# A 6,250-step LSTM on one core: the input projections added by narrow products over four column tiles

## The chip, the cores and the metric

The kernel runs on one core of a Trainium2 chip. The metric is the device time of one execution in microseconds; lower is better. Time before: 31,179.84 us, the median of 3 runs (31,170.26 to 31,184.28).

## The reference

The program is a stack of four layers on 6,250 nodes with 256 features, each added to its input: a weighted graph aggregation, a mixture of eight experts, a graph attention with four heads, and an LSTM over the nodes in order. Only the LSTM matters here:

```python
def _lstm(x, W_ih, W_hh, b_ih, b_hh):
    x_proj = jnp.einsum('btd,gd->btg', x, W_ih) + b_ih + b_hh
    def step(carry, xp):
        h, c = carry
        gates = xp + h @ W_hh.T
        i, f, g, o = jnp.split(gates, 4, axis=-1)
        c = jax.nn.sigmoid(f) * c + jax.nn.sigmoid(i) * jnp.tanh(g)
        h = jax.nn.sigmoid(o) * jnp.tanh(c)
        return ((h, c), h)
    _, hs = jax.lax.scan(step, (h0, c0), jnp.swapaxes(x_proj, 0, 1))
```

The batch is 1, there are 6,250 steps, h and c have 256 elements and each step needs 4 x 256 gate values. All of it is f32. `x_proj` is computed for all steps beforehand.

## The kernel before

The program runs its stages one after the other; the last three are `stage_project` (it writes all projections to HBM), `stage_lstm` and `stage_finish`. The change is in `stage_lstm` alone.

`stage_lstm` gives each engine its own instruction stream, with a hardware loop over N // PER passes (N = 6,250). PER = CH * LU = 2 * 5 = 10 steps are written out in each pass, so there are 625 passes. The order within a step is set by semaphores only; the values they are compared with are computed from the loop's register `i`.

- Layout. The 256 elements of h are held as two columns of 128 (`ht`, index `c`). A gate's 256 values are made as four pieces of 64 (`j`), each piece on a PSUM partition that is a multiple of 32. The gates f, i with g, and o have a PSUM bank each, with two sets of banks that alternate by step (`s = k % 2`).
- SyncE loads the projections of five steps at a time (40 rows of `xp`, two buffers `b`), when TensorE has said by `xp_used` that the buffer has been read.
- TensorE (L1152 to L1180) first adds the projections into the three banks with one product each (L1160). The weights are `sel[:, u, :]`, a matrix of 128 x 128 zeros and ones that picks the rows of step `u`; the moving operand is 64 columns of `xp`. It has ones only in columns 32 j and 32 j + 1. `start=True` makes this product overwrite the bank. Then TensorE waits for h of the step before (`h_ready`) and adds the recurrent part with narrow products: the weights are one or two columns of `ht`, the moving operand is 64 columns of `w`, and `tile_position=(0, 32 * j)` puts each on one of four column tiles of the array. There are 8 for f (L1167), 16 for i and g (L1173) and 8 for o (L1178), and after each group `gates_ready` is counted up.
- VectorE (L1225 to L1243) transposes each bank as blocks of 32 x 32 (L1229 f, L1233 i and g, L1235 o), so that the 64 values of a piece come to lie on partitions, and tells ScalarE by `turned`.
- ScalarE (L1185 to L1199) applies tanh: L1188 to f, L1190 to i and g (written straight into `d`, an input of the scan), L1192 to o. sigmoid is made from tanh, with the weights scaled ahead of the loop.
- GpSimd (L1144 to L1147) multiplies f's tanh with the old cell state into `d` (L1147).
- VectorE then makes the new cell state with one scan over 10 elements (L1239). It first waits for GpSimd (`f_mul`, L1236) and for ScalarE (`ig_act`, L1237).
- ScalarE applies tanh to the cell (L1194) and copies the cell into `d` for the next step (L1195). VectorE writes h (L1242) and counts `h_ready`.
- Every fifth step ScalarE copies five steps of h into `history` (L1199) and counts `kept`, for which VectorE waits ahead of L1233 once in five steps. At the head of a pass ScalarE loads its table (shown at L1188).

Of the kernel before, what the change touches and what calls it, by code (L numbers as in the profile page):

```python
# [16 lines left out]
ALU = mybir.AluOpType  # L17
# [1087 lines left out]
def stage_lstm(nc, sb, sem, g):  # L1105
# [11 lines left out]
    d1, d0 = d[:, 0, 1:2 * SC + 1], d[:, 1, 0:2 * SC]  # L1117
    c_now = cell[:, SC - 1:2 * SC:SC]
    banks_f, banks_ig, banks_o = [[g["ps"][3 * s + k] for s in range(2)] for k in range(3)]
    w_loaded, zeroed, gates_ready, turned, f_act, f_mul, ig_act, scanned, tc_ready, h_ready, kept, xp_used = (sem("ls_" + n) for n in (  # L1120
        "w_loaded", "zeroed", "gates_ready", "turned", "f_act", "f_mul", "ig_act", "scanned", "tc_ready", "h_ready", "kept", "xp_used"))
    xp_in = [sem("ls_xp0"), sem("ls_xp1")]
    PER = CH * LU
    with nc.Block() as block:
        @block.sync
        def _(sp):
            sp.dma_start(w[:, :, :, :].rearrange("p c j n -> p c (j n)"), g["L1_ffn_W_hhT"]).then_inc(w_loaded, 16)
            sp.wait_ge(zeroed, 1)

            def load(b, rows):  # L1130
                sp.dma_start(xp[0:LU * R, b, :], rows.rearrange("u (r n) -> (u r) n", r=R)).then_inc(xp_in[b], 16)

            for b in range(2):
                load(b, g["xp"][b * LU:(b + 1) * LU, :])
            with sp.Fori(0, N // (2 * LU) - 1) as i:
                for b in range(2):
                    sp.wait_ge(xp_used, i * 2 + (b + 1))
                    load(b, g["xp"][ds((i * 2 + (b + 2)) * LU, LU), :])

        @block.gpsimd  # L1140
        def _(pool):
            pool.memset(free[:, :], 0.0).then_inc(kept, 2)
            pool.wait_ge(zeroed, 5)
            with pool.Fori(0, N // PER) as i:  # L1144
                for k in range(PER):
                    pool.wait_ge(f_act, i * PER + (k + 1))
                    nc.gpsimd.tensor_tensor(d1[:, 2:2 * SC:SC], tf[:, :], c_now, ALU.mult).then_inc(f_mul, 1)  # L1147

        @block.tensor
        def _(pe):  # L1150
            pe.wait_ge(zeroed, 5)
            with pe.Fori(0, N // PER) as i:  # L1152
                for k in range(PER):
                    q, u, s = k // LU, k % LU, k % 2
                    b = q % 2
                    if u == 0:
                        pe.wait_ge(xp_in[b], i * (CH // 2 * 16) + (q // 2 + 1) * 16)

                    for bank, lo in ((banks_f[s], HD), (banks_ig[s], 0), (banks_o[s], HD)):
                        x = nc.tensor.matmul(bank[:, 0:HD], sel[:, u, :], xp[:, b, lo:lo + HD], start=True, stop=False)  # L1160
                    if u == LU - 1:
                        x.then_inc(xp_used, 1)
                    pe.wait_ge(h_ready, i * PER + (k + 1))
                    v = (k - 1) % (2 * LU)
                    for c in range(2):
                        for j in range(4):
                            m = nc.tensor.matmul(banks_f[s][32 * j:32 * j + 1, 0:HD], ht[:, v, c, 1:2], w[:, c, j, HD:2 * HD],  # L1167
                                                 start=False, stop=c == 1, tile_position=(0, 32 * j))
                    m.then_inc(gates_ready, 1)
                    for r, lo in ((0, 0), (1, 2 * HD)):  # L1170
                        for c in range(2):
                            for j in range(4):
                                m = nc.tensor.matmul(banks_ig[s][32 * j:32 * j + 2, 0:HD], ht[:, v, c, 1 - r:3 - r], w[:, c, j, lo:lo + HD],  # L1173
                                                     start=False, stop=(r, c) == (1, 1), tile_position=(0, 32 * j))
                    m.then_inc(gates_ready, 1)
                    for c in range(2):
                        for j in range(4):
                            m = nc.tensor.matmul(banks_o[s][32 * j:32 * j + 2, 0:HD], ht[:, v, c, 0:2], w[:, c, j, 3 * HD:4 * HD],  # L1178
                                                 start=False, stop=c == 1, tile_position=(0, 32 * j))
                    m.then_inc(gates_ready, 1)  # L1180

        @block.scalar
        def _(act):
            act.wait_ge(zeroed, 5)
            with act.Fori(0, N // PER) as i:  # L1185
                for k in range(PER):
                    act.wait_ge(turned, i * (3 * PER) + (3 * k + 1))
                    nc.scalar.activation(tf[:, :], tf_cols[:, 0:33:32], ACT.Tanh).then_inc(f_act, 1)  # L1188
                    act.wait_ge(turned, i * (3 * PER) + (3 * k + 2))
                    nc.scalar.activation(d[:, :, 2:3 + SC:SC], ti_cols[:, :].rearrange("p (c m) -> p m c", c=2)[:, 0:2, :], ACT.Tanh).then_inc(ig_act, 1)  # L1190
                    act.wait_ge(turned, i * (3 * PER) + (3 * k + 3))
                    nc.scalar.activation(to[:, :], to_cols[:, 1:34:32], ACT.Tanh)  # L1192
                    act.wait_ge(scanned, i * PER + (k + 2))
                    nc.scalar.activation(tc[:, :], c_now, ACT.Tanh).then_inc(tc_ready, 1)  # L1194
                    nc.scalar.copy(d1[:, 3:2 * SC:SC], c_now)  # L1195
                    if k % LU == LU - 1:
                        v = k % (2 * LU) - (LU - 1)
                        act.wait_ge(h_ready, i * PER + (k + 2))
                        nc.scalar.copy(g["HIST"][:, :, ds(i * PER + (k - LU + 1), LU)], ht[:, v:v + LU, :, 1].rearrange("p u c -> p c u")).then_inc(kept, 1)  # L1199

        @block.vector
        def _(dve):
            vec = nc.vector
            vec.memset(xp[:, :, :], 0.0).then_inc(zeroed, 1)
            vec.memset(sel[:, :, :], 0.0).then_inc(h_ready, 1)
            vec.memset(cell[:, :], 0.0)
            vec.memset(d[:, :, :], 0.0).then_inc(scanned, 1)
            dve.wait_ge(h_ready, 1)
            for j in range(4):
                for r in range(2):  # L1210
                    m = vec.tensor_copy(sel[:, :, 32 * j + r], g["ident"][:, 2 * j + r:2 * j + r + R * (LU - 1) + 1:R])
            m.then_inc(zeroed, 1)
            vec.memset(ht[:, :, :, :], 0.0)
            dve.wait_ge(scanned, 1)
            vec.memset(d1[:, 0:2 * SC:SC], 1.0)
            vec.memset(d0[:, 1:2 * SC:SC], 1.0)
            vec.memset(d0[:, 3:2 * SC:SC], 1.0)
            vec.memset(d0[:, 4:2 * SC:SC], 0.5)
            dve.wait_ge(w_loaded, 16)

            for lo, hi, scale in ((0, 2 * HD, 0.25), (2 * HD, 3 * HD, 0.5), (3 * HD, D, 0.25)):
                v = w[:, :, :, lo:hi].rearrange("p c j n -> p (c j) n")
                vec.tensor_scalar(v, v, scale, None, ALU.mult).then_inc(zeroed, 1)  # L1223
            dve.wait_ge(zeroed, 5)
            with dve.Fori(0, N // PER) as i:  # L1225
                for k in range(PER):
                    s = k % 2
                    dve.wait_ge(gates_ready, i * (3 * PER) + (3 * k + 1))
                    vec.transpose(tf_cols[:, :], banks_f[s][:, 0:HD]).then_inc(turned, 1)  # L1229
                    if k % LU == 0:  # L1230
                        dve.wait_ge(kept, i * CH + (k // LU + 1))
                    dve.wait_ge(gates_ready, i * (3 * PER) + (3 * k + 2))
                    vec.transpose(ti_cols[:, :], banks_ig[s][:, 0:HD]).then_inc(turned, 1)  # L1233
                    dve.wait_ge(gates_ready, i * (3 * PER) + (3 * k + 3))
                    vec.transpose(to_cols[:, :], banks_o[s][:, 0:HD]).then_inc(turned, 1)  # L1235
                    dve.wait_ge(f_mul, i * PER + (k + 1))  # L1236
                    dve.wait_ge(ig_act, i * PER + (k + 1))  # L1237

                    vec.tensor_tensor_scan(cell[:, :], d0, d1, 0.0, ALU.mult, ALU.add).then_inc(scanned, 1)  # L1239
                    dve.wait_ge(tc_ready, i * PER + (k + 1))  # L1240

                    vec.scalar_tensor_tensor(out=ht[:, k % (2 * LU), :, 1], in0=to[:, :], scalar=1.0, in1=tc[:, :],  # L1242
                                             op0=ALU.add, op1=ALU.mult).then_inc(h_ready, 1)  # L1243
# [200 lines left out]
```

## Time and profile before

| | |
|---|---|
| median of 3 runs | 31,179.84 us |
| profiled execution, its own time | 31,181.4 us |
| its span in the profile | 31,179.7 us |
| TensorE products, busy | 26,082.7 us, 84% |
| TensorE weight loads, busy | 21,913.3 us, 70% |
| VectorE, busy | 11,210.6 us, 36% |
| ScalarE, busy | 8,537.5 us, 27% |
| GpSimd, busy | 7,747.7 us, 25% |
| mean granted TensorE clock | 0.631 of full speed |

The profile names TensorE's products PE, its weight loads PEld, VectorE DVE, ScalarE ACT, GpSimd POOL and SyncE SP. An f32 product appears as two product records and two load records. Times in a timeline are microseconds from the start of the span. Busy time of TensorE says little by itself: products are pipelined, so their records overlap, and a record's length holds its way through the array. What counts is the distance between starts, and what the engine waited for. The release of a waiting instruction is inferred from semaphore events, and "issue" is time in which the engine waited for nothing that the profile shows.

### The profile page before, as it was taken

What the parts mean: (1) busy time and instruction counts of PE and PEld (TensorE: products, weight loads), DVE (VectorE), ACT (ScalarE), POOL (GpSimd) and SP (SyncE); (2) the same over time, 40 slices, a digit from 0 to 9 for tenths busy, and PEclk for the clock granted to TensorE, in tenths of its full rate; (3) what the DMA queues carried; (4) which work ended last, traced back from release to release, by engine and by line L of the source; (5) the groups of instructions that cost most, each with busy time, mean ns of one, the idle gap of its engine ahead of it and who ended that gap; (6) DMA issues with size and microseconds to landing.
All of it is one profiled execution on the core that took longest, in us unless ns stands there. A gap on an engine that the chain in (4) does not pass through costs nothing. (4 is left out here: it accounts for less than half of the span.)

```text
span 31179.7 us, 1124934 instructions
## 1 busy us (share of the span) xinstructions
PE 26082.7 (84%) x456492; PEld 21913.3 (70%) x456597; DVE 11210.6 (36%) x40897; ACT 8537.5 (27%) x40793; POOL 7747.7 (25%) x12838
## 2 busy tenths in 40 slices
PE   0002556788777799999999999999999999999998
PEld 0002334333665688888888888888888888888887
DVE  7002333777555333333333333333333333333334
ACT  0000001688111132222222222232222222222322
POOL 1776771677776000000000000000000000000000
PEclk9998778999888655555555555555555555555555
DMA  0002331000333000000000000000000000000000
GB/s 36 1 1 71 104 105 24 7 2 2 97 99 93 33 1 1 1 1 1 1 1 1 1 1 1 1 1 1 1 1 1 1 1 1 1 1 1 1 1 9
DMA packets 370440, 557.74 MB, mean 18 GB/s; under 512 B 177610, under 2 KB 254830, under 8 KB 369006
## 3 DMA queue, kind: packets, MB, share of 16 engines
q0 software_dynamic: 263728, 458.62, 5.9%
q1 hardware_dynamic: 106686, 98.81, 1.0%
q8 instruction: 11, 0.18, 0.0%
q14 instruction: 15, 0.12, 0.0%
HBM read 496.64 MB, written 60.32 MB: 18 GB/s over the span
## 5 line engine op out<-in xcount | busy, mean ns | idle before, releaser
L1160 PE MATMUL banks<-ls_xp,ls_sel 128*128 128x64 f32 x37500 | 9641.6, 430 | 18.2 <-DVE ls_w L1223 18.2
L1160 PEld LDWEIGHTS banks<-ls_xp,ls_sel 128*128 128x128 f32 x37500 | 8466.7, 325 | 1376.1 <-issue 1376.1
L1173 PE MATMUL banks<-ls_w,ls_ht 128*2 128x64 f32 x200000 | 6735.4, 311 | 0.0
L1147 POOL TENSOR_TENSOR ls_d<-ls_tf,ls_cell 128x2 f32<-128x2 f32 x6250 | 1241.9, 199 | 19305.7 <-ACT ls_tf L1188 19305.7
L1173 PEld LDWEIGHTS banks<-ls_w,ls_ht 128*2 128x2 f32 x200000 | 5585.4, 127 | 0.0
L1229 DVE STREAM_TRANSPOSE ls_f_cols<-banks 128x64 f32<-128x64 f32 x6250 | 1561.5, 250 | 7590.1 <-PE banks L1167 7590.1
L1178 PE MATMUL banks<-ls_w,ls_ht 128*2 128x64 f32 x100000 | 4068.7, 311 | 0.0
L436 PE MATMUL banks<-ag_rows,ag_pick 128*128 128x256 f32 x3328 | 1204.8, 526 | 3392.9 <-DMA ag_rows<-y_table,ag_idx 3359.0
L1167 PE MATMUL banks<-ls_w,ls_ht 128*1 128x64 f32 x100000 | 3777.1, 299 | 0.0
L1188 ACT ACTIVATE ls_tf<-ls_f_cols 128x2 f32<-128x2 f32 x6250 | 1286.8, 206 | 8783.7 <-DVE ls_f_cols L1229 8776.7
L436 PEld LDWEIGHTS banks<-ag_rows,ag_pick 128*128 128x128 f32 x3328 | 831.5, 262 | 3765.6 <-DMA ag_rows<-y_table,ag_idx 2759.9
L1178 PEld LDWEIGHTS banks<-ls_w,ls_ht 128*2 128x2 f32 x100000 | 2918.7, 127 | 0.0
L1233 DVE STREAM_TRANSPOSE ls_ig_cols<-banks 128x64 f32<-128x64 f32 x6250 | 1561.5, 250 | 3771.8 <-PE banks L1173 3771.8
L1167 PEld LDWEIGHTS banks<-ls_w,ls_ht 128*1 128x1 f32 x100000 | 1975.0, 103 | 736.4
L1190 ACT ACTIVATE ls_d<-ls_ig_cols 128x4 f32<-128x4 f32 x6250 | 1313.6, 210 | 3849.5 <-DVE ls_ig_cols L1233 3849.5
L1235 DVE STREAM_TRANSPOSE ls_o_cols<-banks 128x64 f32<-128x64 f32 x6250 | 1561.5, 250 | 1105.2 <-PE banks L1178 1105.2
L389 POOL DMA_INDIRECT at_rows<-wh_table,at_idx x1664 | 1743.2, 1048 | 511.1 <-issue 477.3
L389 POOL DMA_INDIRECT mx_rows<-alpha_dst_table,mx_idx x1664 | 1657.0, 996 | 507.7 <-issue 459.8
L329 POOL DMA_INDIRECT rec_table<-st_rec,st_idx x1560 | 1495.1, 958 | 1034.4 <-ACT st_idx L304 559.4
L389 POOL DMA_INDIRECT ag_rows<-y_table,ag_idx x1664 | 1582.0, 951 | 515.8 <-issue 497.9
L1192 ACT ACTIVATE ls_to<-ls_o_cols 128x2 f32<-128x2 f32 x6250 | 1278.3, 205 | 1353.1 <-DVE ls_o_cols L1235 1353.1
L1242 DVE SCALAR_TENSOR_TENSOR ls_ht<-ls_to,ls_tc 128x2 f32<-128x2 f32 x6250 | 1017.3, 163 | 1695.1 <-ACT ls_tc L1194 1695.1
(256 smaller groups left out, 19365.3 us busy)
## 6 DMA issues: line engine op xcount, KB each, us to landing
ag_rows<-y_table,ag_idx POOLq DMA_INDIRECT x1664, 2.7
mx_rows<-alpha_dst_table,mx_idx POOLq DMA_INDIRECT x1664, 2.3
at_rows<-wh_table,at_idx POOLq DMA_INDIRECT x1664, 2.8
projections<-xp_out SPq DMA_DIRECT2D x7, 3584.0 KB, 10.4
rec_table<-st_rec,st_idx POOLq DMA_INDIRECT x1563, 2.1
ls_xp<-projections SPq DMA_DIRECT2D x1250, 20.0 KB
rec_table<-zero POOLq DMA_DIRECT2D x5, 2496.0 KB, 20.9
rec_part<-rec_table SPq DMA_DIRECT2D x5, 2496.0 KB, 19.9
```

Source lines behind the costliest of these rows:

```text
L329: pool.indirect_dma_start(g["rec"][k], bass.IndirectOffsetOnAxis(ap=idx[:, h, u % SH:u % SH + 1], axis=0), recs[:, h, u % SH, :], None).th ...
L389: pool.indirect_dma_start(rows[:, u, :], None, table, bass.IndirectOffsetOnAxis(ap=idx[:, u // HU, u % HU:u % HU + 1], axis=0)).then_inc(g ...
L436: m = nc.tensor.matmul(sums[k], pick[:, u, :], rows[:, u, :], start=u == 2 * k, stop=u == 2 * k + 1)
L1160: x = nc.tensor.matmul(bank[:, 0:HD], sel[:, u, :], xp[:, b, lo:lo + HD], start=True, stop=False)
L1167: m = nc.tensor.matmul(banks_f[s][32 * j:32 * j + 1, 0:HD], ht[:, v, c, 1:2], w[:, c, j, HD:2 * HD], start=False, stop=c == 1, tile_positi ...
L1173: m = nc.tensor.matmul(banks_ig[s][32 * j:32 * j + 2, 0:HD], ht[:, v, c, 1 - r:3 - r], w[:, c, j, lo:lo + HD], start=False, stop=(r, c) == ...
L1178: m = nc.tensor.matmul(banks_o[s][32 * j:32 * j + 2, 0:HD], ht[:, v, c, 0:2], w[:, c, j, 3 * HD:4 * HD], start=False, stop=c == 1, tile_po ...
L1188: nc.scalar.activation(tf[:, :], tf_cols[:, 0:33:32], ACT.Tanh).then_inc(f_act, 1)
L1190: nc.scalar.activation(d[:, :, 2:3 + SC:SC], ti_cols[:, :].rearrange("p (c m) -> p m c", c=2)[:, 0:2, :], ACT.Tanh).then_inc(ig_act, 1)
L1229: vec.transpose(tf_cols[:, :], banks_f[s][:, 0:HD]).then_inc(turned, 1)
L1233: vec.transpose(ti_cols[:, :], banks_ig[s][:, 0:HD]).then_inc(turned, 1)
L1235: vec.transpose(to_cols[:, :], banks_o[s][:, 0:HD]).then_inc(turned, 1)
```

## The change

The product that added the projections of one gate group to a whole bank (128 weight columns) is replaced by four products, one for each column tile, with the one or two weight columns that hold ones: three products a step become twelve. The moving operand is the same 64 columns for all four. Partitions of the bank that no gate value uses are no longer written.

The two semaphores `f_mul` and `ig_act` become one, `scan_in`, which GpSimd and ScalarE both count up; VectorE waits once ahead of the scan, for two counts a step.

```diff
@@ -1117,8 +1117,8 @@
-    w_loaded, zeroed, gates_ready, turned, f_act, f_mul, ig_act, scanned, tc_ready, h_ready, kept, xp_used = (sem("ls_" + n) for n in (
-        "w_loaded", "zeroed", "gates_ready", "turned", "f_act", "f_mul", "ig_act", "scanned", "tc_ready", "h_ready", "kept", "xp_used"))
+    w_loaded, zeroed, gates_ready, turned, f_act, scan_in, scanned, tc_ready, h_ready, kept, xp_used = (sem("ls_" + n) for n in (
+        "w_loaded", "zeroed", "gates_ready", "turned", "f_act", "scan_in", "scanned", "tc_ready", "h_ready", "kept", "xp_used"))
@@ -1144,7 +1144,7 @@
-                    nc.gpsimd.tensor_tensor(d1[:, 2:2 * SC:SC], tf[:, :], c_now, ALU.mult).then_inc(f_mul, 1)
+                    nc.gpsimd.tensor_tensor(d1[:, 2:2 * SC:SC], tf[:, :], c_now, ALU.mult).then_inc(scan_in, 1)
@@ -1156,8 +1156,10 @@
-                    for bank, lo in ((banks_f[s], HD), (banks_ig[s], 0), (banks_o[s], HD)):
-                        x = nc.tensor.matmul(bank[:, 0:HD], sel[:, u, :], xp[:, b, lo:lo + HD], start=True, stop=False)
+                    for bank, m, lo in ((banks_f[s], 1, HD), (banks_ig[s], 2, 0), (banks_o[s], 2, HD)):
+                        for j in range(4):
+                            x = nc.tensor.matmul(bank[32 * j:32 * j + m, 0:HD], sel[:, u, 32 * j:32 * j + m], xp[:, b, lo:lo + HD],
+                                                 start=True, stop=False, tile_position=(0, 32 * j))
@@ -1187,7 +1189,7 @@
-                    nc.scalar.activation(d[:, :, 2:3 + SC:SC], ti_cols[:, :].rearrange("p (c m) -> p m c", c=2)[:, 0:2, :], ACT.Tanh).then_inc(ig_act, 1)
+                    nc.scalar.activation(d[:, :, 2:3 + SC:SC], ti_cols[:, :].rearrange("p (c m) -> p m c", c=2)[:, 0:2, :], ACT.Tanh).then_inc(scan_in, 1)
@@ -1233,8 +1235,7 @@
-                    dve.wait_ge(f_mul, i * PER + (k + 1))
-                    dve.wait_ge(ig_act, i * PER + (k + 1))
+                    dve.wait_ge(scan_in, i * (2 * PER) + (2 * k + 2))
```

## Rows read from the trace of the kernel before

**Rows 1.** Page, part 2: busy tenths and granted clock in 40 slices of the span.

```profile
PE   0002556788777799999999999999999999999998
...
PEclk9998778999888655555555555555555555555555
```

**Rows 2.** One line's records, L1167: count, ns min/median/max, first and last start.

```profile
L1167 PEld LDWEIGHTS banks<-ls_w,ls_ht x100000: 79/106/128, 10473.7 to 31012.2; 128*1 128x1 f32 x200
```

**Rows 3.** Windows: us, then busy us and records by engine, PEclk, DMA share.

```profile
10472.00:10500.00 28.00, 27.81 (x570) 25.01 (x574) 8.16 (x40) 8.02 (x42) 1.59 (x8) 0.50 0.02 4
25000.00:31000.00 6000.00, 6000.00 (x127800) 5388.51 (x127803) 1859.10 (x9127) 1796.14 (x9676) 362.64 (x1825) 0.50 0.00 1
```

**Rows 4.** Timeline of one step: start us, us, engine, line, operation [idle before <-releaser].

```profile
20000.22 1.35 PEld L1160 LDWEIGHTS banks<-ls_xp,ls_sel 128*128 128x128 f32 x6 [0.22 <-issue]
20000.22 1.54 PE L1160 MATMUL banks<-ls_xp,ls_sel 128*128 128x64 f32 x6
...
20000.98 0.16 DVE L1242 SCALAR_TENSOR_TENSOR ls_ht<-ls_to,ls_tc 128x2 f32<-128x2 f32 x1 [0.27 <-ACT ls_tc L1194]
20001.69 0.32 PEld L1167 LDWEIGHTS banks<-ls_w,ls_ht 128*1 128x1 f32 x16
...
20001.97 0.89 PEld L1173 LDWEIGHTS banks<-ls_w,ls_ht 128*2 128x2 f32 x32
...
20002.82 0.47 PEld L1178 LDWEIGHTS banks<-ls_w,ls_ht 128*2 128x2 f32 x16
...
20003.50 0.21 ACT L1190 ACTIVATE ls_d<-ls_ig_cols 128x4 f32<-128x4 f32 x1 [0.65 <-DVE ls_ig_cols L1233]
...
20003.64 0.25 DVE L1235 STREAM_TRANSPOSE ls_o_cols<-banks 128x64 f32<-128x64 f32 x1 [0.18 <-PE banks L1178]
20003.81 0.18 DVE L1239 TENSOR_TENSOR_SCAN ls_cell<-ls_d 128x10 f32<-128x10 f32 x1
20003.93 0.20 ACT L1192 ACTIVATE ls_to<-ls_o_cols 128x2 f32<-128x2 f32 x1 [0.21 <-DVE ls_o_cols L1235]
20004.04 0.19 ACT L1194 ACTIVATE ls_tc<-ls_cell 128x2 f32<-128x2 f32 x1
20004.14 0.18 ACT L1195 COPY ls_d<-ls_cell 128x2 f32<-128x2 f32 x1
20004.26 0.16 DVE L1242 SCALAR_TENSOR_TENSOR ls_ht<-ls_to,ls_tc 128x2 f32<-128x2 f32 x1 [0.27 <-ACT ls_tc L1194]
```

**Rows 5.** Timeline, last stage: TensorE woken by VectorE.

```profile
31145.99 6.73 DVE L1328 SCALAR_TENSOR_TENSOR history<-fi_tmp,fi_nbw,history 128x6250 f32<-128x6250 f32 x1
31152.77 0.93 PEld L1292 LDWEIGHTS banks<-ident,history 128*128 128x128 f32 x5 [88.85 <-DVE history L1328]
```

**Rows 6.** Timeline of a step that begins a pass of the loop.

```profile
20004.96 1.28 ACT L1188 ACT_TABLE_LOAD   x1 [0.21 <-issue]
...
20006.25 0.20 ACT L1188 ACTIVATE ls_tf<-ls_f_cols 128x2 f32<-128x2 f32 x1
...
20006.53 0.20 POOL L1147 TENSOR_TENSOR ls_d<-ls_tf,ls_cell 128x2 f32<-128x2 f32 x1 [3.40 <-ACT ls_tf L1188]
```

**Rows 7.** Timeline of the third step of that pass, VectorE.

```profile
20013.50 0.25 DVE L1235 STREAM_TRANSPOSE ls_o_cols<-banks 128x64 f32<-128x64 f32 x1 [0.18 <-PE banks L1178]
20013.78 0.18 DVE L1239 TENSOR_TENSOR_SCAN ls_cell<-ls_d 128x10 f32<-128x10 f32 x1
```

**Rows 8.** DMA, 10472:10506, queues: packets, MB, share of 16 engines.

```profile
q8 instruction: 6, 0.10, 1.2%
```

**Rows 9.** DMA, 10506:31000, all packets and the queues.

```profile
DMA packets 62300, 25.57 MB, mean 1 GB/s; under 512 B 12460, under 2 KB 62300, under 8 KB 62300
...
q1 hardware_dynamic: 62300, 25.57, 0.4%
```

**Rows 10.** DMA, 10473.3:10475, one instruction packet.

```profile
q8 instruction: 1, 0.02, 4.0%
```

**Rows 11.** DMA issues of the whole span: count, KB, us to landing.

```profile
fi_bl<-in_L_ffn_b_lin SPq DMA_DIRECT2D x1, 1.0 KB, 2.1
```


## The prediction

> **What bounds the kernel now.** The page's slices come first. From slice 14 on TensorE is shown busy without a break and the granted clock stays at 0.5 of full speed [rows 1]. That stretch is the recurrent stage. Its 6,250 steps run at an even pace: the loads of L1167 start from 10473.7 to 31012.2, 20,538.5 us over 6,249 steps, 3.287 us each [rows 2]. The stage is about 20,540 of 31,180 us, and the diff touches nothing else. In both windows of it the granted clock is 0.50, which is 1.2 GHz, although TensorE is recorded as busy throughout [rows 3].
>
> Busy TensorE records do not prove that TensorE is the bound, so the next view is the timeline of one step [rows 4]. The step is a ring: h is written (L1242, starts 20000.98, 0.16 long, so ready at 20001.14), TensorE multiplies it (L1167, L1173, L1178), VectorE transposes, ScalarE applies tanh, VectorE scans, and h is written again at 20004.26 to 20004.42. In this ring one hand-over is slow. h is ready at 20001.14, but the first load that needs it starts at 20001.69. Between them stand the three wide products of L1160, which start at 20000.22 and whose last weight load ends only at 20001.57 (1.54 us of products behind them). So TensorE's own queue holds the ring up for 0.55 us a step; the other waits in the step are dependencies inside it.
>
> The same rows explain why L1160 is dear. It has 6 records a step (each f32 product has two) over 1.54 us, about 0.22 us apart. The 64 narrow records of L1167, L1173 and L1178 take about 1.6 us, that is four records in each 0.107 us (32 loads of L1173 in 0.89 us). Ahead of L1160 the load side also stands idle 0.22 us [rows 4].
>
> **The projections, narrow.** Three products become twelve, so 6 records become 24, in the form of those beside them: 128 rows, 1 or 2 columns, 64 elements, four column tiles in turn. At the pace of L1173 they take 24 x 0.89/32 = 0.67 us. They follow the last L1178 load, at 20003.29 on the scale of rows 4, or 1.60 after the step's first h load, and end their loads at about 2.27. Should the 0.22 us pause remain, 2.49. The ring needs them at 2.78 (next). So they fit behind VectorE and ScalarE with 0.3 to 0.5 us to spare, and the 0.55 us wait goes.
>
> **What the ring then is.** From the first h load to the end of h: 20004.42 less 20001.69 = 2.73 us [rows 4]. To it comes the wake-up of TensorE from a VectorE result. The trace has it in the last stage: L1328 ends at 31145.99 + 6.73 = 31152.72 and the load that waits for it starts at 31152.77, so 0.05 us [rows 5]. New ring: 2.79 against 3.287, a gain of 0.50 us.
>
> Three things take a little back. (1) Before, the instructions behind h were ready and queued when their turn came. Now TensorE starts them as h arrives, from an empty queue. The bounds are nothing and one group of four (0.107); since each group holds the array for 0.107 us anyhow, only the first is late. I take 0.02 us a step, 125 us in all. (2) Once in ten steps ScalarE reloads its table after the history copy: at 20004.96 for 1.28 us, then tf at 20006.25 [rows 6]. Against the end of h at 20004.42 that is 1.83 us. GpSimd's product starts 0.28 after tf and takes 0.20 [rows 6], so it ends at 2.31. Normally the scan will start at 0.05 + (20003.81 - 20001.69) = 2.17 after h. With a wake-up of 0.03 to 0.10 the scan is 0.17 to 0.24 late. It is hidden now; 625 times 0.21 is 130 us. (3) Once in ten steps the scan starts 0.28 us after the start of the o transpose and not 0.17 [rows 7]. Now it ends in the slack ahead of TensorE; then it counts: 625 x 0.1 = 63 us (nothing, if it lands elsewhere).
>
> **One semaphore for the scan.** VectorE loses one wait a step. Now the scan starts 0.10 us after the end of ScalarE's i and g (20003.50 + 0.21 to 20003.81), where L1242, with a single wait, starts 0.03 after ScalarE (20004.04 + 0.19 to 20004.26) [rows 4]. So up to 0.07 us. But the next tanh, L1194, also needs ScalarE: L1192 starts at 20003.93 and L1194 at 20004.04, 0.11 later, while the copy behind L1194, which waits for nothing new, starts 0.10 later [rows 4]. The output gate's tanh then holds L1194, and only 0.01 us is won at most. I take half, 0.005 us a step, 30 us. Queued behind this wait on VectorE is only L1242. The counts are the same (two increments a step), so nothing waits longer.
>
> **Sum.** 6,250 x (3.287 - 2.79) = 3,106; less 125, 130 and 63; plus 30: 2,818 us. The profiled execution took 31,181.4 us and its span is 31,179.7; the median of the runs is 31,179.84, so no correction. 31,180 less 2,818 = 28,362; I say 28,350. The terms' own bounds: all three losses absent and the scan's 0.01 won, 28,010; the queue start at 0.107, 28,900, with little belief in either end. The likeliest case's own range is 28,150 to 28,600.
>
> **Code that no longer fits.** This is the rival that I fear most. The loop body of TensorE is ten steps written out: 6 + 16 + 32 + 16 = 70 loads a step [rows 4] and as many products, so 1,400 instructions a pass. Afterwards it is 88 + 88 = 176 a step, 1,760 a pass. In the first pass the instruction queue q8 fetches 6 packets, 0.10 MB, so blocks of 16 KB [rows 8]; from 10,506 to 31,000 us all 62,300 packets are the q1 queue's, none is an instruction's [rows 9]. TensorE hardly paused in that first pass (27.81 of 28 us busy [rows 3]), so each block must have been fetched ahead of use. The body thus touches about seven blocks, and one more ahead of it was fetched and stayed: eight held. A body 1.26 times as long touches eight and asks for a ninth. No row shows what happens then. If the ninth displaces the first, every pass begins with a fetch that nobody ordered ahead: one packet takes 4.0% of 16 engines over 1.7 us, 1.09 us [rows 10], and a 1 KB transfer takes 2.1 us from issue to landing [rows 11], so 1.1 to 2.1 us. It lies between the last L1178 load (1.60) and the ring's need at 2.78 less 0.67, so 0.5 us are hidden: 0.6 to 1.6 us a pass, 375 to 1,000 us, giving 28,700 to 29,350. If the displaced blocks cascade, the first two are late (only a short piece of the first belongs to the loop) and the others are fetched behind about 4 us of work each: 1,050 to 2,300 us more, 29,400 to 30,650.
>
> The Trainium skill (Advanced Engine Details and Errata, ISA Cache) gives 128 KB for TensorE in lines of 16 KB, 256 instructions. By it the trace's eight blocks are all there is; 1,760 instructions are just under seven lines and can lie across eight, without room for one ahead. The trace agrees with the 16 KB (0.10 MB in 6 packets); no row shows the limit.
>
> **Slower.** The same displacement with no fetch ahead any more: all nine blocks late, 9 x 1.1 to 2.1 = 9.9 to 18.9 us a pass, 5,900 to 11,500 us more, 34,200 to 39,900. It decides from 4.5 us a pass on (2,818/625). Against it speaks that the first pass, where every block was new, ran without a pause.
>
> **No gain.** h might not be waited for as I read it: if a step is held by something else that also takes 3.29 us, the time stays. VectorE and ScalarE are busy for less than a third of the time [rows 3], so little speaks for it.
>
> **A higher clock.** At 2.4 GHz TensorE's 1.6 us a step would shrink, by 0.5 us and more: about 25,200. It stayed at 1.2 GHz through 20 ms recorded as fully busy [rows 1, 3], and afterwards there is less work in the array.
>
> **Chances.** As summed 0.52; one late block a pass 0.2; two late 0.15; slower 0.06; no change 0.02; higher clock 0.02; 0.03 for what I do not see, faster than before. Range for 8 in 10: 28,100 (near the lower bound of the terms) to 29,400 (through the case of one late block). Faster by over 0.2% 0.92, within 0.2% (62 us, about what a measurement of this kernel can tell from no change) 0.02, slower 0.06.
>
> **What the profile would show.** L1160 with 150,000 loads, pairs of 1 or 2 columns, no idle ahead of them; their last load some 0.3 to 0.5 us before h is ready; the first L1167 load 0.05 us after L1242 ends, its idle put down to L1242; a step of about 2.8 us; the clock at 0.5. The table load would show as a late scan once in ten steps. The forecast is wrong if instruction packets number hundreds or thousands and TensorE pauses once in ten steps behind the last L1178; if the narrow records are more than 0.107 us apart per four; or if L1194 starts later after the transposes than now.

## The result and the profile after

The changed kernel takes 30,127.18 us (median of 4 runs, 30,121.59 to 30,131.02). The kernel before took 31,180.40 us beside it (median of 4). The ratio is 0.9663, with a 95% interval of 0.9646 to 0.9679. So it is faster by 1,053 us. The forecast was 28,350 with a range of 28,100 to 29,400: the direction was right, but the time lies outside the range by more than 700 us.

One line bounds the stage best, the one that writes h. In the changed kernel:

```profile
L1243 DVE SCALAR_TENSOR_TENSOR ls_ht<-ls_to,ls_tc x6250: 161/163/165, 10474.9 to 29965.5; 128x2 f32<-128x2 f32 x196
```

In the kernel before:

```profile
L1242 DVE SCALAR_TENSOR_TENSOR ls_ht<-ls_to,ls_tc x6250: 161/163/164, 10476.2 to 31014.6; 128x2 f32<-128x2 f32 x196
```

The stage runs from the first start to the last: 19,491 us, where it was 20,538. That is 31.19 us for a pass of ten steps in place of 32.87. "Stage" means this stretch from here on. The three chips of the experiments differ by up to some 900 us in the other stages, so kernels are compared by it. The kernel before also varies from execution to execution (29,819 to 31,187 us on one of these chips, 31,520 to 32,070 on another), and its mean clock rises as its time falls (0.688 of full speed at 29,819 us, 0.632 at 31,187), while the changed kernel's four executions lie within 10 us.

The page of the changed kernel, parts 2, 3 and 5 (line, form, count, busy us, mean ns, idle us before it and its releaser):

```profile
PE   0002556688777655555555555555555555555555
...
PEclk9999777899888788888888888888888888888888
...
q8 instruction: 5629, 92.23, 1.4%
...
L1161 PEld LDWEIGHTS banks<-ls_xp,ls_sel 128*2 128x2 f32 (+1 forms) x150000 | 2995.0, 91 | 4191.5 <-issue 4174.2
...
L1169 PEld LDWEIGHTS banks<-ls_w,ls_ht 128*1 128x1 f32 x100000 | 1617.0, 87 | 4426.4 <-DVE ls_ht L1243 4188.1
```

Three things differ from [rows 1, 9]. The granted clock stands at 0.8 in the page's tenths over the stage (0.88 on average from 20000 to 25000 us), where it was 0.5. TensorE is half idle. And the instruction queue, silent before, carries 5,629 packets. The idle time of L1169 is put down to h, as forecast, but L1161 has 4,191.5 us of idle time that ends by "issue", that is by nothing the profile shows. The prediction named this as what would make it wrong: instruction packets by the thousand.

The weight loads of TensorE around one jump of the loop, from its timeline:

```profile
20009.75 0.15 PEld L1180 LDWEIGHTS banks<-ls_w,ls_ht 128*2 128x2 f32 x10 [1.16 <-issue]
...
20011.03 0.22 PEld L1169 LDWEIGHTS banks<-ls_w,ls_ht 128*1 128x1 f32 x16 [0.74 <-DVE ls_ht L1243]
...
20015.44 0.22 PEld L1161 LDWEIGHTS banks<-ls_xp,ls_sel 128*1 128x1 f32 x15 [3.52 <-issue]
20018.34 0.19 PEld L1161 LDWEIGHTS banks<-ls_xp,ls_sel 128*2 128x2 f32 x9 [2.68 <-issue]
20018.47 0.48 PEld L1169 LDWEIGHTS banks<-ls_w,ls_ht 128*1 128x1 f32 x16
```

TensorE stops in the middle of straight code for 1.16 us. At the head of the loop it stops for 3.52 us, runs 15 loads, and stops for 2.68 us more. The step with the jump takes 8.42 us on average, from h to h. The DMA view of ten passes (20000 to 20311.9) has the fetches; its columns are packets, MB, share of 16 engines:

```profile
q8 instruction: 90, 1.47, 2.1%
```

Nine blocks of 16 KB in each pass, one every 311.9 / 90 = 3.47 us. All nine of them are fetched anew each time: 625 x 9 = 5,625.

The windows of the changed kernel over one pass and the start of the next (busy us and records by engine, then the granted clock):

```profile
14998.60:15022.50 23.90, 13.32 (x764) 10.86 (x752) 9.39 (x45) 9.32 (x48) 1.78 (x9) 1.00 0.03 7
15022.50:15029.40 6.90, 3.48 (x117) 2.92 (x121) 0.97 (x5) 1.14 (x6) 0.20 (x1) 0.51 0.02 5
```

The clock is at 2.4 GHz for 23.9 us of a pass. It falls to 1.2 GHz within the step of the jump, in which TensorE stands idle twice, stays there for 6.8 us and then returns; so it is in 624 passes. In [rows 3] it was 0.50 throughout. So two things happened that the forecast had left out or priced low, and they pull in opposite directions. The experiments take them apart.

### The profile page after: what moved, and what is told of

It reads as the page before. It is cut to its first block and busy times, and to the rows that moved or that the text cites. A ratio compares the mean times of both kernels' runs of the same rounds, so it can differ in the third digit from the quotient of the medians.

```text
span 30129.3 us, 1349934 instructions
## 1 busy us (share of the span) xinstructions
PE 16500.0 (55%) x568992; PEld 12458.3 (41%) x569097; DVE 11297.1 (37%) x40897; ACT 8897.0 (30%) x40793; POOL 7742.5 (26%) x12838
## 3 DMA queue, kind: packets, MB, share of 16 engines
q8 instruction: 5629, 92.23, 1.4%
## 5 line engine op out<-in xcount | busy, mean ns | idle before, releaser
L1161 PE MATMUL banks<-ls_xp,ls_sel 128*2 128x64 f32 (+1 forms) x150000 | 4256.1, 237 | 3807.9 <-issue 3785.6
L1175 PE MATMUL banks<-ls_w,ls_ht 128*2 128x64 f32 x200000 | 4678.8, 234 | 353.9 <-issue 347.2
L1169 PE MATMUL banks<-ls_w,ls_ht 128*1 128x64 f32 x100000 | 2986.5, 234 | 3202.7 <-DVE ls_ht L1243 3072.4
L1161 PEld LDWEIGHTS banks<-ls_xp,ls_sel 128*2 128x2 f32 (+1 forms) x150000 | 2995.0, 91 | 4191.5 <-issue 4174.2
L1180 PE MATMUL banks<-ls_w,ls_ht 128*2 128x64 f32 x100000 | 3264.0, 232 | 1157.9 <-issue 1157.9
L1175 PEld LDWEIGHTS banks<-ls_w,ls_ht 128*2 128x2 f32 x200000 | 3643.7, 92 | 482.5 <-issue 478.1
L1169 PEld LDWEIGHTS banks<-ls_w,ls_ht 128*1 128x1 f32 x100000 | 1617.0, 87 | 4426.4 <-DVE ls_ht L1243 4188.1
L1180 PEld LDWEIGHTS banks<-ls_w,ls_ht 128*2 128x2 f32 x100000 | 2153.5, 91 | 1393.1 <-issue 1393.1
L1194 ACT ACTIVATE ls_to<-ls_o_cols 128x2 f32<-128x2 f32 x6250 | 1276.9, 204 | 1731.9 <-DVE ls_o_cols L1237 1674.1
```

Source lines behind the costliest of these rows:

```text
L1161: x = nc.tensor.matmul(bank[32 * j:32 * j + m, 0:HD], sel[:, u, 32 * j:32 * j + m], xp[:, b, lo:lo + HD], start=True, stop=False, tile_pos ...
```

## The experiments

My theory: the body, 1,413 instructions of TensorE before and 1,773 after, no longer fits with the block fetched ahead; each block is then fetched again each pass, and the clock gives back a part. Rival: the halts belong to the narrow products or to the semaphore.

### Where the code lies: 40, 20, 28, 32 and 56 instructions ahead of the loop

Dummy products ahead of the loop, each four TensorE instructions, move the whole body in memory by some instructions and leave it as it is. They write a bank that the loop overwrites. With 10 of them (40 instructions):

```diff
             pe.wait_ge(zeroed, 5)
+            for _ in range(10):
+                nc.tensor.matmul(banks_o[1][0:1, 0:HD], ht[:, 0, 0, 1:2], w[:, 0, 0, 0:HD], start=True, stop=True, tile_position=(0, 0))
             with pe.Fori(0, N // PER) as i:
```

> The changed kernel with ten dummy narrow products (40 instructions) ahead of the loop, which only move the loop's code. Theory (displacement): TensorE keeps eight blocks of 256 instructions, the block fetched ahead included. The changed body lay across eight blocks and called for a ninth, 5,625 packets in 625 passes. Moved by 40 instructions it lies across seven and calls for an eighth: instruction packets of the stage fall to some 6 to 8, the waits once per block go, and the step is 2.11 us if the clock stays at 2.4 GHz (about 23,900 us in all) or about 2.8 us if it falls back to 1.2 GHz (about 28,300 us). Rival (length): the body is too long wherever it lies; nothing moves, 30,100 us and some 5,600 packets.

Measured: 24,515.0 us (24,511.67 to 24,525.06, 4 executions), where the kernel before took 29,819 to 31,187 us on the same chip. The stage is 13,866 us. Its h line, in the view of one line's records:

```profile
L1245 DVE SCALAR_TENSOR_TENSOR ls_ht<-ls_to,ls_tc x6250: 161/163/164, 10490.7 to 24357.0; 128x2 f32<-128x2 f32 x196
```

Its page, parts 2 and 3:

```profile
PEclk9999877789999888799999999999999999999998
...
q8 instruction: 13, 0.21, 0.0%
```

Forty instructions that do nothing took 5,625 us off the stage (19,491 less 13,866, on two chips; the equal number of packets is chance). From 10515 to 24300 us not one instruction packet is left. The timeline of this kernel has a step at each clock, and the seam of two passes:

```profile
10650.38 0.16 DVE L1245 SCALAR_TENSOR_TENSOR ls_ht<-ls_to,ls_tc 128x2 f32<-128x2 f32 x1 [0.27 <-ACT ls_tc L1198]
10650.59 0.32 PEld L1171 LDWEIGHTS banks<-ls_w,ls_ht 128*1 128x1 f32 x16 [0.89 <-DVE ls_ht L1245]
...
10652.15 0.68 PEld L1163 LDWEIGHTS banks<-ls_xp,ls_sel 128*1 128x1 f32 x24
...
10653.16 0.16 DVE L1245 SCALAR_TENSOR_TENSOR ls_ht<-ls_to,ls_tc 128x2 f32<-128x2 f32 x1 [0.30 <-ACT ls_tc L1198]
...
19999.92 0.16 DVE L1245 SCALAR_TENSOR_TENSOR ls_ht<-ls_to,ls_tc 128x2 f32<-128x2 f32 x1 [0.27 <-ACT ls_tc L1198]
...
20001.34 0.21 ACT L1194 ACTIVATE ls_d<-ls_ig_cols 128x4 f32<-128x4 f32 x1 [0.24 <-DVE ls_ig_cols L1237]
...
20001.58 0.18 DVE L1242 TENSOR_TENSOR_SCAN ls_cell<-ls_d 128x10 f32<-128x10 f32 x1
...
20002.03 0.16 DVE L1245 SCALAR_TENSOR_TENSOR ls_ht<-ls_to,ls_tc 128x2 f32<-128x2 f32 x1 [0.27 <-ACT ls_tc L1198]
...
20009.05 1.28 ACT L1192 ACT_TABLE_LOAD   x1 [0.21 <-issue]
...
20010.35 0.20 ACT L1192 ACTIVATE ls_tf<-ls_f_cols 128x2 f32<-128x2 f32 x1
...
20010.86 0.18 DVE L1242 TENSOR_TENSOR_SCAN ls_cell<-ls_d 128x10 f32<-128x10 f32 x1 [0.89 <-POOL ls_d L1147]
```

At 1.2 GHz a step takes 10653.16 - 10650.38 = 2.78 us; at 2.4 GHz it takes 20002.03 - 19999.92 = 2.11. The low clock comes for 3.4 us in every 89 or so and goes again. Of its 156 falls in the stage 155 begin in the second step of a pass, right behind the step with the table load, in which TensorE waits 1.73 us for h and not 0.89. The windows show one such dip and what follows:

```profile
10650.30:10653.70 3.40, 2.84 (x104) 2.56 (x108) 1.14 (x6) 0.93 (x7) 0.20 (x1) 0.50 0.00 0
10653.70:10715.10 61.40, 39.79 (x2460) 34.02 (x2448) 29.77 (x140) 29.88 (x149) 5.58 (x28) 1.00 0.01 2
```

With `range(5)` (20 instructions):

> The same with five dummy products (20 instructions). Theory (displacement): that is not enough to leave the first block, nine blocks are still asked for, 5,600 packets and about 30,100 us. Rival (the dummy products themselves change the clock or the start of the stage): it moves as the kernel with ten does, about 24,000 to 28,300 us.

Measured: 30,303.12 us, stage 19,654, 5,629 instruction packets. So it isn't the dummies as such that help. On this one chip 20 more of them, from 20 to 40, are worth 5,788 us of stage.

With `range(7)` (28) and `range(8)` (32), on one chip with the next:

> Seven dummy products (28 instructions) ahead of the loop. In the trace of the changed kernel the loop meets its block borders at its instructions 30, 286, 543, 798, 1053, 1309 and 1566. Theory (displacement): 28 leave a rest of the first block in the loop, so nine blocks are still asked for: some 5,620 instruction packets, 31 us a pass. Rival (any shift of this size helps, or the cost goes away gradually): fewer packets than with 20.

> Eight dummy products (32 instructions): four more. Theory: the loop's head now lies behind the border, eight blocks suffice, some 13 instruction packets in the whole run, 22.2 us a pass. Rival: as with 28.

Measured: 31,313.0 us with a stage of 19,783 for 28, and 25,392.5 us with 13,867 for 32. The instruction queue on the page of the one with 28:

```profile
q8 instruction: 5629, 92.23, 1.2%
```

and of the one with 32:

```profile
q8 instruction: 13, 0.21, 0.0%
```

The halts of the changed kernel show block borders at loop instructions 30, 543, 798, 1053, 1309 and 1566, some 256 apart, or twice that. The border between the first two, at 286, is passed without a halt, in the stretch at 1.2 GHz. With 28 more instructions ahead, two instructions of the loop still lie before the first border, and the body touches eight blocks. With 32 it begins behind a border and touches seven. So seven blocks and one fetched ahead stay, eight and one do not. The stage differs by 5,916 us between the two, on one chip; with 28 the whole program took longer than the one execution of the kernel before beside it (30,317.61 us). By this the kernel should also lose its place at the other end:

With `range(14)` (56):

> Fourteen dummy products (56 instructions). Theory: the loop of some 1,775 instructions, moved so far, now ends behind the next border (seven blocks are 1,792 instructions, 18 more than the body, and the head stands 25 or so behind its border), so nine blocks are asked for again: 5,620 packets, 31 us a pass. Rival (only the start of the loop matters, or the dummy products themselves help): as with 40, 22.2 us a pass.

Measured: 25,411.9 us, stage 13,874. This missed. The DMA view from 11360 to 11395 us has 7 packets, and from 11395 to 11445 it has these:

```profile
q8 instruction: 9, 0.15, 1.4%
```

After that none comes until 25000. Nine blocks were fetched once more and then the loop held. Here the last of eight blocks has only 1,773 + 26 - 7 x 256 = 7 instructions of the loop, and a fetch ahead of a ninth may not be asked for before the jump; no run tests that, and it stays open.

### Fifty steps written out

```diff
-CH = 2
+CH = 10
```

> The changed kernel with fifty steps written out a pass (CH = 10), so about 35 blocks a pass that nothing could keep. Theory (a fetch takes about 3.4 us from its trigger to its use and is triggered when the block before it is entered): 3.47 us a block as in the ten-step body, 35 blocks and one late jump a pass, 2.43 to 2.5 us a step, about 25,900 us and 4,400 packets. So it is faster than the ten-step body, since only the jump back costs more, and that once in fifty steps. Rival (each block is fetched only when it is missed, the full time exposed): 3.05 + 3.4 us a block, 4.5 us a step, about 38,700 us.

Measured: 27,594.96 us, stage 16,945 us, 2.71 us a step. The page has these instruction queues:

```profile
q8 instruction: 4629, 75.84, 1.2%
q14 instruction: 1510, 12.37, 0.2%
```

The body cannot be kept at all, and TensorE fetches 37 blocks in each of the 125 passes, one every 16,945 / 4,625 = 3.66 us. If straight code hid its fetches, most steps would take 2.11 us. They don't: 256 instructions last 256/177 x 2.11 = 3.05 us at 2.4 GHz (177 a step), less than the 3.47 to 3.66 us from block to block. That it is still faster than the changed kernel fits with a jump, with its two halts in a row, and a table load only once in fifty steps; no run parts these. My expectation of 25,900 had 35 blocks a pass at 3.47 us; there were 37 at 3.66. The other engines' bodies grew too: their instruction queue q14 carries 1,510 packets where the changed kernel has 15, and ScalarE, too, waits by "issue" ahead of its table load, 3.2 us on average and not 0.21. How much of the 3.66 us is theirs, no run shows.

### The semaphore alone, at 1.2 GHz

The changed kernel with the projections as they were:

```diff
-                    for bank, m, lo in ((banks_f[s], 1, HD), (banks_ig[s], 2, 0), (banks_o[s], 2, HD)):
-                        for j in range(4):
-                            x = nc.tensor.matmul(bank[32 * j:32 * j + m, 0:HD], sel[:, u, 32 * j:32 * j + m], xp[:, b, lo:lo + HD],
-                                                 start=True, stop=False, tile_position=(0, 32 * j))
+                    for bank, lo in ((banks_f[s], HD), (banks_ig[s], 0), (banks_o[s], HD)):
+                        x = nc.tensor.matmul(bank[:, 0:HD], sel[:, u, :], xp[:, b, lo:lo + HD], start=True, stop=False)
```

> The kernel before with the one semaphore for the scan alone. Theory: TensorE's queue sets the end of a step (it starts on h 0.55 us late), so an earlier scan only lengthens that wait; within 0.2% of 31,180 us, scan start to end of ScalarE's i and g from 0.10 to 0.03 us or held by the o transpose. Rival (the scan's wait is on the path): up to 0.07 us a step, 440 us less.

Measured: six executions of 31,182.0, 24,369.6, 24,372.0, 24,375.5, 31,180.2 and 24,368.2 us. The two near 31,180 have a mean clock of 0.63 over the span, the four others 0.95. The profiled one has 0.63, and its stage is 20,538.3 us, equal to before within 0.1 us. Its timeline:

```profile
20000.85 1.35 PEld L1160 LDWEIGHTS banks<-ls_xp,ls_sel 128*128 128x128 f32 x6 [0.22 <-issue]
...
20000.98 0.25 DVE L1235 STREAM_TRANSPOSE ls_o_cols<-banks 128x64 f32<-128x64 f32 x1 [0.18 <-PE banks L1178]
20001.16 0.14 DVE L1238 TENSOR_TENSOR_SCAN ls_cell<-ls_d 128x10 f32<-128x10 f32 x1
...
20001.60 0.16 DVE L1241 SCALAR_TENSOR_TENSOR ls_ht<-ls_to,ls_tc 128x2 f32<-128x2 f32 x1 [0.31 <-ACT ls_tc L1194]
...
20002.32 0.32 PEld L1167 LDWEIGHTS banks<-ls_w,ls_ht 128*1 128x1 f32 x16
```

At 1.2 GHz the semaphore saves no time here: the scan still starts 0.18 us after the start of the o transpose (0.17 in [rows 4]) and 0.11 after ScalarE's i and g; h is ready at 20001.76 and TensorE takes it up at 20002.32, behind L1160. One thing did change. Every step from h to h takes 3.28 or 3.29 us, where in the kernel before 624 take 3.39 and 624 take 3.18: the late scan of [rows 7] is gone with the second wait. The other four executions say more. With three wide products and no narrow one for the projections, the whole program took 24,370 us, less than any kernel with narrow ones on this chip (24,512 at least). No profile was taken of those, only their times and clocks.

### The clock, started high under the wide products

The kernel before, with 480 narrow dummy products ahead of the loop, which write a bank that it overwrites:

```diff
+            with pe.Fori(0, 60):
+                for c in range(2):
+                    for j in range(4):
+                        nc.tensor.matmul(banks_o[1][32 * j:32 * j + 1, 0:HD], ht[:, 0, c, 1:2], w[:, c, j, 0:HD],
+                                         start=True, stop=True, tile_position=(0, 32 * j))
             with pe.Fori(0, N // PER) as i:
```

> The kernel before, its wide products kept, with 60 turns of eight dummy narrow products ahead of its loop, some 20 us of TensorE work. Theory (two levels that each hold themselves): the stage of the kernel before runs at whichever clock level it got; brought to 2.4 GHz ahead of the first step it stays there, because its three wide products then take half the time and end before h is ready: a step of 2.1 to 2.2 us, 24,400 us, as four of six runs of the kernel with one semaphore had. Rival (the wide products push the clock down): it falls to 1.2 GHz soon after the loop begins, 31,180 us.

Measured: 31,882.2 us (31,103 to 32,004), where the kernel before took 31,520 to 32,070 us on this chip. The windows, before and after 11864.70 us:

```profile
11373.20:11864.70 491.50, 406.91 (x14993) 341.81 (x14986) 214.88 (x1010) 213.04 (x1070) 39.89 (x202) 1.00 0.01 2
11864.70:20000.00 8135.30, 8135.30 (x173286) 7306.20 (x173290) 2515.99 (x12376) 2424.93 (x13117) 488.50 (x2475) 0.50 0.00 1
```

2.4 GHz is held for 491.5 us, the dummies' time included. Then the clock falls to 1.2 GHz and stays there to the stage's end, 19.9 ms. Nothing in the instruction stream changes at 11864.70. So my theory, that the level keeps itself once it is high, missed: it held for 201 steps and no longer. In the first stretch most steps take 2.18 us (161 of the 201); the timeline there:

```profile
11600.31 0.74 PEld L1165 LDWEIGHTS banks<-ls_xp,ls_sel 128*128 128x128 f32 x6
...
11600.51 0.21 ACT L1195 ACTIVATE ls_d<-ls_ig_cols 128x4 f32<-128x4 f32 x1 [0.24 <-DVE ls_ig_cols L1238]
11600.73 0.20 ACT L1197 ACTIVATE ls_to<-ls_o_cols 128x2 f32<-128x2 f32 x1
11600.82 0.18 DVE L1244 TENSOR_TENSOR_SCAN ls_cell<-ls_d 128x10 f32<-128x10 f32 x1
...
11601.27 0.16 DVE L1247 SCALAR_TENSOR_TENSOR ls_ht<-ls_to,ls_tc 128x2 f32<-128x2 f32 x1 [0.27 <-ACT ls_tc L1199]
...
11601.48 0.22 PEld L1172 LDWEIGHTS banks<-ls_w,ls_ht 128*1 128x1 f32 x16 [0.43 <-DVE ls_ht L1247]
```

At 2.4 GHz the wide loads end at 11600.31 + 0.74 = 11601.05, 0.38 us before h is ready at 11601.43. Of the two clocks, the wait that the change removes is there only at 1.2 GHz.

### Only f narrow

Four narrow products for f, one wide product each for i with g and for o; the body is then 1,533 instructions.

```diff
-                    for bank, m, lo in ((banks_f[s], 1, HD), (banks_ig[s], 2, 0), (banks_o[s], 2, HD)):
-                        for j in range(4):
+                    for bank, m, lo in ((banks_f[s], 1, HD), (banks_ig[s], 128, 0), (banks_o[s], 128, HD)):
+                        if m == 128:
+                            x = nc.tensor.matmul(bank[:, 0:HD], sel[:, u, :], xp[:, b, lo:lo + HD], start=True, stop=False)
+                        else:
+                            for j in range(4):
...
```

> The changed kernel with four narrow products for f alone; i with g and o keep a wide product. That is 152 loads and products a step, 1,530 a pass, which by the displacement theory end before the block that calls for the ninth: some 6 instruction packets in the stage and none later. At 2.4 GHz a step of 2.11 us and about 24,500 us, at 1.2 GHz TensorE has 0.6 us of wide loads less its pauses and the step is about 3.1 us, 30,000 us. Rival (the number of products in a pass, not the blocks, brings the fetches): 1,500 packets or more and waits of over 5 us at each pass.

Measured: 25,266.9 us (25,262 to 25,268, 3 executions), a ratio of 0.7982 to the kernel before on the same chip, 95% interval 0.7903 to 0.8061. The h line:

```profile
L1246 DVE SCALAR_TENSOR_TENSOR ls_ht<-ls_to,ls_tc x6250: 161/163/165, 11359.4 to 25095.2; 128x2 f32<-128x2 f32 x196
```

The stage is 13,736 us, the shortest that was profiled. The step is 2.11 us; the whole program fetches 12 blocks; the clock falls to 0.5 for 3.4 us in every 900 or so and returns each time. With two wide products it returns; with three it did not, in any profile here (there is none of the four executions at 24,370 us).

### Two semaphores, and 32 columns, in the kernel that fits

The kernel with 40 instructions ahead, with the two old semaphores (the lines that count them up change with it):

```diff
...
-                    dve.wait_ge(scan_in, i * (2 * PER) + (2 * k + 2))
+                    dve.wait_ge(f_mul, i * PER + (k + 1))
+                    dve.wait_ge(ig_act, i * PER + (k + 1))
```

> The changed kernel moved by 40 instructions, with the two semaphores of the kernel before. In it TensorE starts on h as soon as h is there, so the scan's start counts. Theory (the output gate's tanh holds the next one): the scan is 0.07 us later, a step 0 to 0.07 us longer, up to 440 us over the 24,515 us of the kernel with one semaphore; at 2.4 GHz the o transpose comes early, so I expect most of the 0.07. Rival (the transposes hold the scan): 24,515 us within 0.2%.

Measured: 25,780.5 us (25,779 to 25,783, 4 executions), stage 14,249 against 13,866. The step takes 2.18 us in place of 2.11. At 2.4 GHz the one semaphore is thus worth 0.07 us in most steps and 383 us in all; the step with the table load takes 2.95 us with either. 2.18 us is also the step of the kernel before in its 491.5 us at 2.4 GHz, so at that clock the narrow products are worth nothing.

The kernel with 40 instructions ahead, with 32 weight columns in each narrow product:

```diff
-                    for bank, m, lo in ((banks_f[s], 1, HD), (banks_ig[s], 2, 0), (banks_o[s], 2, HD)):
+                    for bank, m, lo in ((banks_f[s], 32, HD), (banks_ig[s], 32, 0), (banks_o[s], 32, HD)):
```

> The changed kernel moved by 40 instructions, each of the twelve products with all 32 weight columns of its tile. The code has the same length. Theory: the loads take a little longer (32 columns instead of 1 or 2), they lie in the slack ahead of h, and the clock stays as it was: 24,500 to 24,600 us. Rival (wide weights are what held the kernel before at 1.2 GHz): the clock falls to 0.5 in the stage, 28,300 us and more.

Measured: 25,400.8 us, stage 13,866, the same. That the other columns are left out is neither what saves time nor what lifts the clock.

## Why the prediction was right in its direction and wrong in its size

- **TensorE no longer waits behind the wide products.** Right at 1.2 GHz, the clock it was worked out for: h wakes L1171 0.05 us after it is ready (10650.38 + 0.16 to 10650.59), as forecast.
- **24 narrow records in 0.67 us.** Right: 0.68 at 1.2 GHz.
- **The ring of 2.79 us.** Right: 2.78 at 1.2 GHz. (The working's 2.73 + 0.05 is 2.78 too; 2.79 was a rounding.) The 0.02 for an empty queue was not there.
- **The table load, 0.21 us a pass.** The mechanism is right, the size holds only at the low clock. At 2.4 GHz the rest of the step shrinks and the load of 1.28 us does not. The step with it takes 2.95 us against 2.11, which is 0.84 x 625 = 525 us in the kernel that fits, and nearly all its falls of the clock come right behind it. No run takes it out. In the changed kernel it is hidden in the halts at the jump.
- **The third step's late scan, 63 us.** Wrong: it went with the second wait. With one semaphore no step has it, at 1.2 GHz under wide products (all steps 3.28 or 3.29 us) or at 2.4 GHz, where the scan starts 0.03 us after the end of i and g's tanh (20001.34 + 0.21 to 20001.58).
- **One semaphore, at most 0.01 us, since the output gate's tanh holds L1194.** At 1.2 GHz the size is right, but the 0.10 us ahead of the scan is not the second wait's: it is there with one semaphore too (0.11), where the scan keeps its 0.17 or 0.18 us behind the o transpose. At 2.4 GHz the second wait does hold the scan (11600.51 + 0.21 to 11600.82, 0.10 us, against 0.03 with one), and the output gate's tanh no longer ends after the scan (with one semaphore both end at 20001.76). There the one semaphore is worth the 0.07 that the prediction had measured and then set aside.
- **No price for code in the likeliest case, and "hidden behind about 4 us of work" in the rival: the step that failed.** The prediction counted the blocks rightly (eight touched, a ninth asked for) but put the cost of that at nothing in its sum. In its rival it bounded the price of a fetch by its packet (1.09 us) and by a 1 KB transfer (2.1 us). Neither holds what passes between the wish for a block and its first instruction.
- **What the runs showed in its place.** At the jump the wait is 3.52 us for the first block and 2.68 us more for the second. In straight code a block comes every 3.5 us or so, while 256 instructions last 3.05 us at 2.4 GHz. The first pass before could not show it: it ran at 1.2 GHz [rows 3] with 1,413 instructions in ten steps of 3.29 us, so a block lasted 256/141 x 3.29 = 6.0 us. The forecast's 4 us for the changed body holds at 1.2 GHz only (256/177 x 2.78 = 4.0), where block border 286 indeed brings no halt. So all nine are fetched again each pass, with halts at the jump and at six of the seven borders: 5,625 us of stage (19,491 less 13,866), 9.0 us a pass. The case of two late blocks, with a chance of 0.15, had 1.7 to 3.7 us a pass; that of all nine late, with 0.06, had 9.9 to 18.9. The 9.0 us include the slower steps of the low clock behind each jump and leave out the table load that the jump hides.
- **"It stayed at 1.2 GHz through 20 ms recorded as fully busy, and afterwards there is less work in the array": wrong.** This is the other step that failed. In every kernel with narrow projections that was profiled the clock returns to 2.4 GHz after each fall. That case had a chance of 0.02. Nor was the level before a fixed one: of six executions of one kernel with three wide products, two ran low and four high.

In sum: a stage of 20,538 - 2,818 = 17,720 was forecast. The clock takes 3,854 from it (13,866 in the kernel that fits) and the fetches add 5,625: 19,491. The forecast's error of 1,770 us is the difference of two larger ones, and the right direction is in part luck: in this sum the fetches alone outweigh the forecast gain of 2,818, and only the clock turns the sign. The 1,053 us also stand against executions of the kernel before at 31,170 to 31,184 us; its 29,819 us on another chip is below every execution of the changed kernel.

At 2.4 GHz the mechanism that was argued for is worth nothing. What the narrow products bring beyond it, as far as these executions show, is a clock that comes back: three wide ones gave 31,180 us in two executions and 24,370 in four of one and the same kernel, while with one of the three made narrow all three executions, no more, were within 6 us.

The Trainium skill (Advanced Engine Details and Errata, section ISA Cache) gives TensorE 128 KB in lines of 16 KB, or 256 instructions. By that there are eight lines, and the runs agree: seven blocks and one ahead stay (13 packets), eight and one are fetched again to the last (5,629), with the kernel with 56 instructions as an exception that no run settles.

Two versions beat both kernels: the changed one with 40 instructions ahead of its loop (stage 13,866) and the one with only f narrow (13,736). The second has the smaller body: 1,533 instructions touch at most seven blocks wherever they lie, so it should not hang on their place; one place was run. Of its 130 us, the dips can account for some 110 (an estimate from their counts): the first has 156, and 3.4 us at 2.78 a step instead of 2.11 lose about 0.8 us each; the second has 15.

Open: why the clock stays low under three wide products and returns under two; whether it stayed high or returned in the four executions at 24,370 us, of which no profile is kept; why the loop across eight blocks with 7 instructions in the last one holds.

## What to carry to other kernels

Count a hardware loop's instructions on each engine before more is written out in it, and look at the instruction queue afterwards: packets that grow with the passes mean a body that is fetched again, at a price that neither the packet's length nor a first pass at a low clock tells. When a stage is recorded as fully busy at half the clock, ask which of its waits would exist at the full one before an edit is credited with removing them. Compare a candidate also with a plain shift of its code: here the step from 28 to 32 idle instructions was worth 5,900 us.

## What the runs showed of the hardware

- A block of TensorE's code is 16 KB (90 packets, 1.47 MB). It took 3.5 us at a jump to a block that was gone, 2.7 us more for the next, and 3.47 us a block on average where every block was late (3.66 in the fifty-step body).
- Four instructions more or less ahead of a loop (28 or 32) decided between 19,783 and 13,867 us of the same stage.
- TensorE kept 1.2 GHz for 19.9 ms while recorded as busy without a break, after 491.5 us at 2.4 GHz with the same instructions. In kernels with narrow projections it fell too, but was back after 3.4 us (6.8 behind the halts of a jump).
- In the kernel that fits, 155 of 156 falls began right behind the step in which TensorE had waited 1.73 us for h.
- A second semaphore wait ahead of one VectorE instruction cost 0.07 us in most steps at 2.4 GHz: the scan starts 0.10 us after ScalarE with two and 0.03 with one.
